# A fused two-layer block with routed experts: shared feed-forward moved out of the loop, last batch in half banks and token tiles, and three programs joined into one

## The chip, the cores and the metric

One NeuronCore of one Trainium2 chip runs the whole kernel in one launch. The metric is the device time of that launch in microseconds (us), median over runs. All data are fp32 except a few small bf16 tiles that hold exact integers or split values. The engines are named as in the profile: PE is TensorE (PEld its weight loads), DVE is VectorE, ACT is ScalarE, POOL is GpSimd, SP is SyncE. SP, ACT and POOL also issue DMAs from queues of their own.

## The reference, cut to what matters

The input `x` is 8 batches of 256 tokens with 512 features. Four blocks follow each other; `ln` is a layer norm without weights.

```python
x = x + tanh(g_xattn[0]) * L0_xattn(ln(x), ctx, ctx)   # retention: scores summed over all 8 batches
x = x + tanh(g_ffn[0])   * L0_ffn(ln(x))               # shared FF + one expert times a weight
x = x + tanh(g_xattn[1]) * L1_xattn(ln(x), ctx, ctx)   # softmax attention, 8 heads
x = x + tanh(g_ffn[1])   * L1_ffn(ln(x))               # 64 experts, top 6, capacity 256
```

In the first block `A = maximum(abs(masked.sum(axis=0)), 1)` needs the scores of every batch before any batch can go on. The last block, on which most of the change bears, is

```python
su = x_flat @ w_shared_up
y_s, g_s = split(su, 2, axis=-1)
shared = silu(g_s) * y_s @ w_shared_down
scores = sigmoid(x_flat @ w_gate)
_, topk_idx = top_k(scores, 6)
w = take_along_axis(scores, topk_idx, -1); w = w / w.sum(-1, keepdims=True)
# place of each (token, expert) pair among the rows of its expert, in token order; rows past 256 are dropped
out_r[e] = (silu(g_r) * v_r) @ w_down[e],  g_r, v_r = split(x_disp[e] @ w_up[e], 2)
routed = sum over the 6 experts of a token of w * out_r
result = shared + routed
```

## The kernel before

The work is three programs one after the other, each with tiles of its own and a barrier of all engines behind it.

**`setup_and_scores`** normalises `x` batch by batch, stores the transposed result and the values to DRAM (`xnT_d`, `v_d`), accumulates the scores of all batches in PSUM and makes `AT`, the masked `A`. SP loads the weights behind the last loads of this part: `weights(...)`.

**`main_loop`** takes a batch through four streams of units: F (first block's output, gate, and the first feed-forward), T (softmax attention), R (routing and the shared feed-forward of the last block) with its sends. Every engine walks one written list, `ORDER`, in which `T.S0+1` means that unit T.S0 lags one step behind: in step s it works on batch s-1. There are 8 steps with a new batch and 3 more in which the lagging streams finish (lags go up to 3). Every engine runs its own units of that list strictly in order, with semaphores between engines. PSUM has one group of four banks, `quad`, three banks in rotation, `work`, and one bank `pV`. `quad` holds a chunk of attention scores: first in the units T.S0 to T.S7 (PE makes 128x2048 scores, DVE takes the row maxima, L888), then in T.Q0 to T.Q7 (PE makes them again, transposed and shifted, ACT takes the exponentials into `probs`, L721). T.V are the products with the values (L1178). POOL sums the exponentials of a group of four chunks (T.sum, L624, three sums of four instructions each, twice a batch), a matmul T.Z turns that into row sums, and DVE scales (T.A), POOL adds (T.add). R then does: stats, norm, turn, gates (routing logits), sigmoid, hot (top 6 as one-hot), pos (places by a matmul), slots, places (addresses); POOL sends 12 groups of 128 rows per batch to the experts' row table `xs_d` (R.x, L644) and 12 groups of row numbers to `ids_d` (R.send, L658). The shared feed-forward is R.up (eight matmuls of 128x256, L1057), R.shared (one exponential on ACT, four DVE instructions, L935 to L938), R.down (two matmuls of 128x512, L1221, and two DVE instructions, L943), and SP stores the sum to `acc_d`. ACT also issues the 56 fills that clear `xs_d` and `y_d`.

**`experts`** takes 32 pairs of experts: rows and weights are loaded four pairs ahead (L1290, L123, L124), PE transposes the rows (L1435), makes the up product (L1447) and the down product (L1458), ACT and DVE evict, and POOL scatters the results to `y_d` by the numbers in `ids_d` (L1340). POOL first sends the last batch's 12 groups of numbers (L1329); SP waits for them, loads `e_ids` (L1311) and only then the rows and weights of pair 4. At the end, for each of 16 token tiles, SP loads two halves of 768 KB from `y_d` (L1306), DVE adds six scaled slices into `acc` (L1415), and ACT stores the tile (L1374).

## Time and profile before

| | us |
|---|---|
| median of 3 runs (lowest, highest) | 1253.87 (1252.85, 1258.54) |
| the profiled execution's own time | 1244.85 |
| its span, first to last instruction | 1243.1 |
| PE busy | 1003.2 (81%) |
| DVE busy | 707.4 (57%) |
| POOL busy | 611.1 (49%) |
| ACT busy | 300.8 (24%) |

The profile is of one execution, whose time lies 0.7% below the median of the others. Busy time is summed over the whole span; the stages have different limits, so the stages are read one by one. POOL's share does not count the time in which it issues a DMA beyond the instruction itself. An fp32 matmul of the program shows as two PE instructions in the trace.

### The profile page before, as it was taken

To read this page: it belongs to the slowest core of one execution; us is meant where nothing else is said; L and a number is where in the kernel's file an instruction comes from. 1 tells how busy PE (TensorE), PEld (TensorE's weight loads), DVE (VectorE), ACT (ScalarE), POOL (GpSimd) and SP (SyncE) were. 2 spreads that over 40 slices of the span, in tenths; PEclk is the share of its full clock that TensorE was granted. 3 is DMA by queue.
4 is the path that set the end of the run, shared out by engine and by line. 5 is a ranking of instruction groups with operands and counts; after the bars stand their busy time and mean duration, and the time that the engine had idled before them with its cause. 6 is when DMAs were issued, how large, how long until landed. Compare 5 with 4: busy or idle time off the path is not lost. (4 is left out here: it accounts for less than half of the span.)

```text
span 1243.1 us, 16070 instructions
## 1 busy us (share of the span) xinstructions
PE 1003.2 (81%) x5966; PEld 562.1 (45%) x5966; DVE 707.4 (57%) x1241; ACT 300.8 (24%) x390; POOL 611.1 (49%) x588
## 2 busy tenths in 40 slices
PE   6947989999999999999999966742888989899000
PEld 6945545454555545545555422231454555455000
DVE  3312353778868778778687785450333333333598
ACT  2411022223232222242322312200223232323000
POOL 1100004626777668667776687875443444344100
PEclk9978999999999999999999986765999999999655
DMA  4892049487380652712403015035789899994796
GB/s 183 304 356 85 1 163 385 180 294 282 136 305 12 233 196 102 273 67 102 136 2 127 27 51 187 0 131 200 251 304 330 291 344 296 328 297 172 281 419 283
DMA packets 103834, 252.24 MB, mean 203 GB/s; under 512 B 14016, under 2 KB 14400, under 8 KB 102993
## 3 DMA queue, kind: packets, MB, share of 16 engines
q1 hardware_dynamic: 50896, 137.92, 32.1%
q10 hardware_dynamic: 31872, 62.92, 13.3%
q0 software_dynamic: 20992, 50.42, 10.6%
q8 instruction: 46, 0.75, 0.3%
q14 instruction: 28, 0.22, 0.1%
HBM read 125.26 MB, written 134.33 MB: 209 GB/s over the span
## 5 line engine op out<-in xcount | busy, mean ns | idle before, releaser
L1340 POOL DMA_INDIRECT y_d<-e_eo,e_ids x128 | 124.8, 975 | 158.5 <-DVE e_eo L1395 126.8
L624 POOL TENSOR_TENSOR t_psum<-t_psum,t_probs 128x512 f32<-128x512 f32 x128 | 162.8, 1302 | 50.8 <-ACT t_probs L721 47.8
L888 DVE TENSOR_REDUCE t_nmx<-quad 128x4 f32<-128x2048 f32 x64 | 146.5, 2289 | 62.6 <-PE quad L1138 62.4
L721 ACT ACTIVATE t_probs<-quad 128x2048 f32<-128x2048 f32 x64 | 120.2, 1877 | 174.6 <-PE quad L1163 174.4
L644 POOL DMA_INDIRECT xs_d<-r_norm,r_xaddr x96 | 95.5, 995 | 28.0 <-issue 27.7
L658 POOL DMA_INDIRECT ids_d<-r_tokk,r_addr x84 | 82.7, 984 | 42.5 <-DVEq L1003 20.9
L1160 PE MATMUL quad<-b_qry,b_key 32*128 32x512 f32 x512 | 78.8, 687 | 19.9 <-ACT t_probs L721 13.6
L1389 DVE TENSOR_TENSOR e_hT<-e_pU,e_gate 128x256 f32<-128x256 f32 x32 | 13.6, 425 | 140.5 <-ACT e_gate L1356 98.2
L1435 PE MATMUL e_pT<-ident,e_xg 128*128 128x128 f32 x512 | 72.4, 286 | 22.9 <-DMA e_xg<-xs_d 22.4
L624 POOL TENSOR_TENSOR t_psum<-t_probs 128x512 f32<-128x512 f32 x64 | 82.3, 1320 | 11.7 <-ACT t_probs L721 9.7
L1138 PE MATMUL quad<-b_key,b_qry 32*128 32x512 f32 x512 | 74.7, 654 | 16.4 <-DVE t_nmx L888 13.2
L605 POOL TENSOR_TENSOR f_rstd<-f_veps,mhalf 128x2 f32<-128x2 f32 x24 | 17.0, 707 | 144.3 <-DVE f_veps L789 144.3
L1435 PEld LDWEIGHTS e_pT<-ident,e_xg 128*128 128x128 f32 x512 | 56.7, 144 | 61.0 <-issue 26.8
L1178 PE MATMUL t_pV<-t_probs,b_cT 128*32 128x512 f32 x512 | 68.2, 620 | 0.0
L1384 DVE COPY e_xT<-e_pT 128x512 f32<-128x512 f32 x64 | 44.1, 689 | 41.0 <-PE e_pT L1435 39.6
L1057 PE MATMUL work<-f_normT,wupT 128*128 128x256 f32 x256 | 61.3, 395 | 0.0
L1057 PE MATMUL work<-b_xnT,wg 128*128 128x256 f32 x256 | 59.7, 387 | 1.6 <-DVE f_zT L808 1.6
L1395 DVE COPY e_eo<-e_pD 128x512 f32<-128x512 f32 x64 | 44.3, 692 | 28.5 <-PE e_pD L1458 25.8
L1049 PE MATMUL work<-wo,f_zT 128*128 128x512 f32 x128 | 58.6, 601 | 1.3 <-issue 1.3
L1049 PE MATMUL work<-wexp,f_normT 128*128 128x512 f32 x128 | 58.7, 601 | 0.5 <-issue 0.5
L1049 PE MATMUL work<-wdnT,f_hT 128*128 128x512 f32 x128 | 58.8, 604 | 0.0
L1057 PEld LDWEIGHTS work<-f_normT,wupT 128*128 128x128 f32 x256 | 48.9, 196 | 17.0 <-issue 10.6
(185 smaller groups left out, 1657.8 us busy)
## 6 DMA issues: line engine op xcount, KB each, us to landing
xs_d<-zero ACTq DMA_DIRECT2D x32, 1024.0 KB, 8.1
e_xg<-xs_d SPq DMA_DIRECT2D x32, 1024.0 KB
y_d<-zero ACTq DMA_DIRECT2D x24, 1024.0 KB
e_xg<-y_d SPq DMA_DIRECT2D x16, 768.0 KB, 11.5
e_eo<-y_d SPq DMA_DIRECT2D x16, 768.0 KB, 11.7
a_x<-in_x SPq DMA_DIRECT2D x8, 512.0 KB, 4.5
a_cT<-in_ctxT SPq DMA_DIRECT2D x8, 512.0 KB, 3.6
v_d<-a_val SPq DMA_DIRECT2D x8, 512.0 KB, 2.7
```

Source lines behind the costliest of these rows:

```text
L624: ins = g_.tensor_tensor(psum0[:, q, :], first[:, q, :], probs[s % NP][:, q, :], ALU.add)
L644: g_.indirect_dma_start(out=xs_d, out_offset=bass.IndirectOffsetOnAxis(ap=xaddr[b % 2][:, t, k:k + 1], axis=0), in_=normR[b % 2][:, t, :], ...
L658: g_.indirect_dma_start(out=ids_d, out_offset=bass.IndirectOffsetOnAxis(ap=addr[b % 2][:, t, k:k + 1], axis=0), in_=tokk[b % 2][:, t, k:k ...
L721: A(probs[s % NP][:, :, :], quad[:, :, :], ACT.Exp, scale=SCALE1).then_inc(W["exp_ok"], 1)
L888: V.tensor_reduce(nmx[g][:, m, :], quad[:, :, :], axis=AX.X, op=ALU.max, negate=True).then_inc(W["mx_ok"], 1)
L1049: ins = mm(dst, lhs[:, k, t * P:(t + 1) * P], w[:, k, :], start=(k == 0), stop=(k == KC - 1))
L1057: ins = mm(dst[:, j * S:(j + 1) * S], w[:, k, o * P:(o + 1) * P], rhs[:, k, :], start=(k == 0), stop=(k == KC - 1))
L1138: ins = mm(quad[:, q, :], qry[b % 2][r, g, m * P:(m + 1) * P], key[b % 2][r, g, :], start=True, stop=True)
L1160: mm(quad[:, q, :], key[b % 2][r, g, n * P:(n + 1) * P], qry[b % 2][r, g, :], start=True, stop=False)
L1178: ins = mm(pV[q * HD:(q + 1) * HD, :], cT[:, n, r:r + HD], probs[s % NP][:, q, :], start=(n == 0), stop=(n == KC - 1))
L1340: g_.indirect_dma_start(out=y_d, out_offset=bass.IndirectOffsetOnAxis(ap=ids[:, HC * p + n:HC * p + n + 1], axis=0), in_=eo[u][:, n, :], i ...
L1435: last = tr(pT[t][:, k * P:(k + 1) * P], xg[u][:, HT * e + t, k * P:(k + 1) * P], ident[:, :])
```

## The change

1. **Shared feed-forward out of the loop.** The units R.up, R.shared and R.down leave the list. The transposed normalised rows of batches 0 to 6 are kept in DRAM (`nrT_d`, unit R.keep, a 512 KB store per batch) and loaded back (7 x 512 KB) near the end. Eight units L.up0 to L.up7 at the end of the list make the up products into the `quad` banks; ACT applies Silu and DVE multiplies (one instruction each per batch) into `shT`. The down product is made in the final sum: one 128x512 matmul per token tile.
2. **The final sum.** PE takes the first three of the six slices of a tile: it multiplies them by diagonal matrices (`diag`, made by ACT from the identity, three 128x128 instructions per tile) into the PSUM bank in which the shared product is. DVE takes the other three and then adds the bank.
3. **The last batch.** Steps 0 to 5 follow a new `ORDER`; what comes after is a second written list, `ENDING`. In it the attention of batch 7 works on halves of `quad` (L.S0a, L.S0b, ...: two banks each), the sums of its exponentials are made by PE in a bank of `work` (four more matmuls per L.V) and not by POOL, and its routing goes by token tile (L.stats0, L.norm0, ..., L.places1, L.rows0, L.rows1).
4. **One program.** The three parts share one block and one address map (`arena`, `put`, `banks`) without barriers; waits on single semaphores take their place. Parts that stand for the barriers: ACT and DVE wait for the accumulated rows' stores (`accst`) before the experts, SP waits for the last sends (`xscat`, `scat`) before it loads rows, PE for `shT_ok` before the first up product.
5. **Order on the queues.** SP issues the loads for batch 0 (`load_front`) ahead of the weights, and all weights but the routing ones ahead of the stores of batches 6 and 7. The sends of a batch's row numbers wait for a semaphore of their own (`ids_ok`), and those of batch 6 stand behind the last rows of batch 7.

The diff, cut to its core:

```diff
+            start = nc.sbuf_base
+            sb("arena", [P, 123 * 256], ctx=mid)
+            put = lambda n, shape, kb, d=F32: nc.alloc_sbuf_tensor_at(n, shape, d, offset=start + int(1024 * kb))
+            banks = mid.enter_context(nc.psum_tensor("banks", [P, 2 * KC, D], F32))
...
+            parts = [setup_and_scores(nc, io, outer, mid, everything)]
+            parts.append(main_loop(nc, io, outer, mid, everything))
+            parts.append(experts(nc, io, out, outer, mid, everything))
+            with nc.Block() as block:
...
+        sp.dma_start(mask[:, :, :, :], io["mask"]).then_inc(mask_in, 16)
+        for u in range(2):
+            sp.wait_ge(stored[u], 2 * 16)
+        v["load_front"](sp, 0)
+        weights("gate_in", "wg", "gamma", "beta")
+        weights("wo_in", "wo")
+        weights("ffn_in", "wg0", "wupT", "wdnT", "wexp")
+        last = NB // 2 - 1
...
+T.sum1a/5 T.sum1b/5 T.V2/5 T.Z0/5 T.V3/5 T.add0/5 T.Q7/5 T.A0/5 F.out0/7 T.S0/6 F.keys/7 F.out1/7 F.stats/7 T.V4/5 T.S1/6 F.norm/7 T.V5/5
...
+T.Q5/6 R.places/5 F.down1/7 T.V2/6 T.Q6/6 T.Z0/6 T.V3/6 T.Q7/6 F.stats3/7 F.norm3/7 T.V4/6 T.sum1a/6 T.V5/6 T.A0/6 L.S0a/7 L.S0b/7 T.V6/6
+T.sum1b/6 L.S1a/7 L.S1b/7 T.sum1c/6 L.S2a/7 L.S2b/7 R.x3/4 T.add0/6 L.S3a/7 L.S3b/7 T.Z1/6 L.P0/7 L.S4a/7 R.acc/5 R.acc/6 L.S4b/7 R.send0/5
+R.x0/5 T.V7/6 L.M0/7 L.S5a/7 L.S5b/7 L.Q0a/7 T.A1/6 L.Q0b/7 L.S6a/7 T.add1/6 L.S6b/7 R.stats/6 R.send1/5 L.Q1a/7 R.norm/6 L.Q1b/7 L.S7a/7
+R.x1/5 R.x2/5 L.S7b/7 R.send2/5 R.turnA/6 R.send3/5 R.turnB/6 L.Q2a/7 L.Q2b/7 R.gates/6 L.add0/7 L.M1/7 L.Q3a/7 L.P1/7 L.V0/7 R.sigmoid/6
+L.V1/7 R.x3/5 R.hot/6 L.A0/7 L.Q3b/7 R.slots/6 L.stats0/7 R.places/6 L.V2/7 L.Q4a/7 R.x0/6 L.V3/7 L.Q4b/7 L.norm0/7 R.x1/6 L.Q5a/7 L.A1/7
+R.pos/6 L.Q5b/7 L.add1/7 L.sigmoid0/7 L.stats1/7 L.hot0/7 L.V4/7 L.norm1/7 R.x2/6 L.Q6a/7 L.slots0/7 L.Q6b/7 R.keep/5 L.V5/7 R.x3/6 L.Q7a/7
+L.Q7b/7 L.places0/7 R.keep/6 L.V6/7 L.rows0/7 L.rows1/7 L.V7/7 R.send0/6 L.turn0/7 R.send1/6 R.send2/6 L.sigmoid1/7 L.gates0/7 L.pos0/7
+L.turn1/7 R.send3/6 L.gates1/7 L.up0/7 L.up1/7 L.hot1/7 L.pos1/7 L.up2/7 L.up3/7 L.up4/7 L.up5/7 L.up6/7 L.up7/7 L.slots1/7 L.places1/7
...
+        def r_keep(b):
+            sp.wait_ge(W["x4T_ok"], 2 * b + 2)
+            sp.dma_start(nrT_d[b, :, :].rearrange("p (k s) -> p k s", k=KC), normRT[:, :, :]).then_inc(W["nr_kept"], 16)
...
+        def last_weighted(s):
...
+                for q in range(G):
+                    r = (g * G + q) * HD
+                    mm(pV[q * HD:(q + 1) * HD, :], cT[:, n, r:r + HD], probs[s % NP][:, q, :], start=(n == 0), stop=(n == KC - 1))
+                for q in range(G):
+                    ins = mm(z[q * HD:(q + 1) * HD, :], ones32[:, :], probs[s % NP][:, q, :], start=(n == 0), stop=(n == KC - 1))
...
+        def shared_up(c):
+            def stage(b):
+                if c == 0:
+                    pe.wait_ge(W["nr_in"], 16 * LB)
+                    pe.wait_ge(W["exp_ok"], 8 * b + 16)
                 pe.wait_ge(W["x4T_ok"], 2 * b + 2)
+                since(pe, W["shT_ok"], c - G + 1)
+                by_features(quad[:, c % G, :], wsu, normRT if c == LB else nrT[c], 0).then_inc(W["su_mm"], 1)
+            return stage
...
+        for u in range(2):
+            sp.wait_ge(W[f"xscat{u}"], 16 * T * TOPK * (NB // 2))
+        sp.wait_ge(W["pv_mm"], 8 * NB)
+        for p in range(XB):
+            load_rows(p)
+        for u in range(2):
+            sp.wait_ge(W[f"scat{u}"], 16 * T * TOPK * (NB // 2 - u))
+        sp.wait_ge(ids_sent, 16 * T * TOPK)
...
+        def halves(i):
+            j = 2 * i
+            u = j % (XB + OB)
...
+            since(pe, part_ok, i - HC + 1)
+            mm(pD[i % HC][:, :], shT[:, i // T, (i % T) * P:(i % T + 1) * P], wsd[:, :], start=True, stop=False)
+            pe.wait_ge(part_in[u], 16 * uses(j, XB + OB))
+            pe.wait_ge(diag_ok, i + 1)
+            for k in range(HALF):
+                last = mm(pD[i % HC][:, :], diag[i % 2][:, k, :], parts[u][:, k, :], start=False, stop=(k == HALF - 1))
+            last.then_inc(half_mm, 1)
```

## Rows read from the trace of the kernel before

**Rows 1.** Busy time by stretch: start:end, length, busy us, granted clock, DMA share, GB/s.

```profile
78.60:147.90 69.30, 49.89 (x177) 34.53 (x178) 12.48 (x29) 5.80 (x10) 1.99 (x4) 0.81 0.30 116
...
384.70:467.70 83.00, 81.48 (x477) 42.43 (x473) 63.71 (x116) 23.39 (x26) 59.95 (x55) 1.00 0.46 165
...
632.80:717.50 84.70, 83.09 (x492) 43.02 (x492) 66.05 (x118) 24.63 (x28) 62.08 (x57) 1.00 0.17 57
717.50:798.00 80.50, 59.60 (x344) 22.33 (x336) 52.02 (x85) 20.94 (x18) 63.76 (x56) 0.75 0.25 92
798.00:866.30 68.30, 21.71 (x65) 12.93 (x61) 23.75 (x61) 3.74 (x6) 46.01 (x46) 0.58 0.35 129
866.30:1161.20 294.90, 254.65 (x1792) 147.72 (x1792) 100.01 (x160) 85.19 (x160) 132.62 (x136) 0.98 0.83 284
1161.20:1243.10 81.90, 0.00 (x0) 0.00 (x0) 70.83 (x96) 0.00 (x0) 0.00 (x0) 0.50 0.89 359
```

**Rows 2.** Timeline at the end of setup: start us, us, engine, line, operation.

```profile
77.08 1.02 DVE L336 TENSOR_SCALAR AT<-mask 128x1024 f32<-128x1024 f32 x2
...
78.60 0.33 SPq L561 DMA_DIRECT2D b_val<-v_d  x1
...
89.94 1.43 PE L1067 MATMUL work<-b_val,AT 128*128 128x128 f32 x5 [16.50 <-DMA b_val<-v_d]
```

**Rows 3.** Timeline of PE in one step of the loop.

```profile
393.00 3.72 PE L1057 MATMUL work<-r_normT,wsu 128*128 128x256 f32 x16
396.65 1.14 PE L1138 MATMUL quad<-b_key,b_qry 32*128 32x512 f32 x8
...
419.13 1.02 PE L1221 MATMUL work<-wsd,r_shT 128*128 128x512 f32 x2
420.08 1.14 PE L1160 MATMUL quad<-b_qry,b_key 32*128 32x512 f32 x8
...
454.99 3.70 PE L1049 MATMUL work<-wdnT,f_hT 128*128 128x512 f32 x8
```

**Rows 4.** Groups of POOL's instructions in one step, 384.7 to 467.7 us.

```profile
L624 POOL TENSOR_TENSOR t_psum<-t_psum,t_probs 128x512 f32<-128x512 f32 x16 | 20.5, 1312 | 4.8 <-ACT t_probs L721 4.5
L644 POOL DMA_INDIRECT xs_d<-r_norm,r_xaddr x12 | 12.1, 1008 | 3.3 <-issue 3.3
```

**Rows 5.** Costliest groups of the page: busy us, mean ns, idle before.

```profile
L888 DVE TENSOR_REDUCE t_nmx<-quad 128x4 f32<-128x2048 f32 x64 | 146.5, 2289 | 62.6 <-PE quad L1138 62.4
```

**Rows 6.** Timeline of DVE, routing of the last batch, first and last row.

```profile
823.59 0.46 DVE L949 TENSOR_SCALAR r_eg<-r_eg 128x128 f32<-128x128 f32 x1 [2.86 <-issue]
...
835.36 0.48 DVE L1005 TENSOR_SCALAR comb_all<-r_small,r_wsum,tg_f 128x6 f32<-128x6 f32 x2 [0.15 <-issue]
```

**Rows 7.** Timeline, last send of rows to second expert pair, and one stretch.

```profile
850.13 0.98 POOL L644 DMA_INDIRECT xs_d<-r_norm,r_xaddr  x1 [0.30 <-issue]
...
856.00:858.00 2.00, 0.00 (x0) 0.00 (x0) 0.00 (x0) 0.00 (x0) 0.00 (x0) 0.50 0.00 0
...
860.50 2.84 SPq L1290 DMA_DIRECT2D e_xg<-xs_d  x4
...
866.26 3.87 PE L1435 MATMUL e_pT<-ident,e_xg 128*128 128x128 f32 x16 [22.44 <-DMA e_xg<-xs_d]
871.00 3.67 PE L1447 MATMUL e_pU<-e_xT,wo 128*64 128x256 f32 x32 [0.88 <-issue]
...
883.84 0.44 PE L1447 MATMUL e_pU<-e_xT,wupT 128*64 128x256 f32 x2
```

**Rows 8.** The final sum: timeline, one stretch of 5 us, time to landing of the output.

```profile
1158.58 0.98 POOL L1340 DMA_INDIRECT y_d<-e_eo,e_ids  x1 [0.30 <-issue]
...
1165.89 6.21 DVE L1415 SCALAR_TENSOR_TENSOR e_acc<-e_xg,comb_all,e_acc 128x512 f32<-128x512 f32 x8 [11.20 <-DMA e_xg<-y_d]
...
1185.00:1190.00 5.00, 0.00 (x0) 0.00 (x0) 4.73 (x7) 0.00 (x0) 0.00 (x0) 0.50 1.02 419
...
DMA to landing us min/median/max: 2.0/6.7/7.5
```

2378 lines of the change are left out of this document (1286 added, 1092 removed), and 3 rows, old and new, of the table RELEASES.

## Prediction

> **What bounds the kernel now.** I cut the busy time into stretches that follow the program [rows 1]; what to see is which engine is full in each. In a full step of the loop (384.7 to 467.7) PE is busy 81.5 of 83.0 us at the full clock: PE is the bound, DVE (64) and POOL (60) are not. Step 0 (78.6 to 147.9) and the drain (717.5 to 866.3) are different: PE is busy 49.9, 59.6 and 21.7 us of 69.3, 80.5 and 68.3, and the granted clock averages 0.81, 0.75 and 0.58, so part of that busy time is at the 1.2 GHz level. In the drain POOL is the busiest engine (110 of 149 us). The experts (866.3 to 1161.2) keep PE busy 86% and the DMA engines 83%. The final sum has DVE busy 71 of 82 us and PE idle. All sums are made against the profiled execution: 1244.85 us, of which the span is 1243.1.
>
> **Term 1, end of setup.** DVE finishes `AT` at 78.1, but PE's first product starts at 89.94, because the first load of a batch is issued at 78.60 behind the weights [rows 2]. In the change this load stands ahead of the weights, and its wait (stores of batches 0 to 3) was met long before, so nothing queues behind it for long. 89.9 - 78.2 = 11.7 us go. The new step 0 transposes before it makes the first gate product (3.65 us), which so far covered the wait for the norm: I give back 2 us, half of it. **-9.7** (bounds -12 and -5).
>
> **Term 2, shared feed-forward out of the steps.** R.up holds PE from 393.00 to 396.65, 3.65 us; R.down from 419.13 to 420.08, 0.95 us, twice [rows 3]: 5.55 us per batch. By the end of F of batch 7 (717.5) these units had run for batches 0 to 4 in the old list. Adding up the units on either list up to that point with such rows gives PE 24.5 us less in the new one. What DVE sheds (some 5 us per batch) is off the path. The added stores (7 x 512 KB out and in) meet DMA engines that are busy 0.17 to 0.53 here; R.keep makes SP wait for the transposed rows in mid-step, and behind it stands the load for the next batch, wanted some 40 us later: nothing. POOL is busy 60.0 us in a step [rows 1], and each of its 24 sends holds it 0.30 us beyond its 0.98 [rows 7]: 67 us, which the change leaves as they are, against a step of 82.8 - 5.55 = 77.2. PE stays the bound. **-24.5** (bounds -28, and +7 if the new order leaves more gaps). F of batch 7 then ends at 717.5 - 9.7 - 24.5 = 683.
>
> **Term 3, the drain.** Before, it is 153.5 us from 717.5 to the first up product at 871.0 [rows 7]. In it engines and DMA queues also stand still before the barrier opens at 860.5: nothing is moved from 856 to 858. After, three queues have to be followed.
> POOL: after F of batch 7 its list holds three sums of four instructions (12 x 1.31 = 15.7 [rows 4]), 11 groups of three sends (33 x 1.28 = 42.2) and four adds and three roots (7, from the 5 us that a step's two adds and four roots leave of its 60) before the second tile's root: 65 us. So that root is not before 683 + 66 = 749.
> DVE: its list up to the last attention scaling adds up to 48 us, of which 16 half maxima at half of 2.29 us [rows 5]. PE must fit 16 half-scores, 16 half-exponentials and the V units of 2 us around them, part of it at 1.2 GHz; I take 59 us for the last V, 742, and scaling and add bring it to POOL's bound. From 749: norm, hot, slots, places of tile 0 and sigmoid of tile 1 on DVE. Two tiles took 12 us [rows 6], one tile then some 8 us: 758. The second tile's hot ends at 761.
> PE: gates of the second tile 755.5, then two shared up products, 7.3 us, stand ahead of L.pos1: it runs at 764. Slots, places: 767. Six sends, 7.7: 775. Landing and load of the first rows: 2.7 (1158.58 to 1161.2) and 5.7 (860.5 to 866.2) give 783. But PE has eight up products of 3.65 = 29.2 us behind 755.5, and starts them cold: 787. Transposes, 2 us: the first expert product at **789**. 789 - 683 = 106 against 153.5: **-47.5**. Bounds: POOL's queue alone (88 us to the last row, plus 10.4) ends at 782, -54; with all eight up products at 1.2 GHz, as PE ran much of this stretch before, +29, so -18.
>
> **Term 4, the experts.** Before, they start at half clock: the first interval between up products is 12.8 us (871.0 to 883.84), later ones average 8.9 ((1158.58 - 883.84) / 31). After, dense products stand right ahead: -4. Against it: the numbers of batches 6 and 7, 24 sends of 1.28, are sent only after the last rows, so SP is free to load pair 4 at 775 + 31 + 2 = 808. PE wants those rows in pair 3, at about 789 + 3 x 8.9 + 4 = 820, the load takes 5.7: hidden, but the DMA engines start with less lead, and the share was 0.83 over the whole stage. +1. **-3** (bounds -4, and +8 if the transfers run late for a while).
>
> **Term 5, the final sum.** Before: 84.5 us from the last scatter (1158.58) to the end. DVE does six slices in 4.67 us per tile (1165.89 on: 8 instructions of 0.75 in 6.21), 95% busy. The DMA engines, though, are also full: share 1.02, 419 GB/s [rows 8]. The loads (32 x 768 KB) and stores (16 x 256 KB) are 29.4 MB, 70.1 us at that rate: begun at 1161.2 they end at 1231.3 at best. DVE's new work is four instructions of 0.75 to 0.78, 3.1 us per tile, PE's 4 products of 0.92 = 3.7 us [rows 3], both under 4.4 us of transfers. After the last landing three slices, the bank's add (3.2 us), issue and landing of a store (2.4): 1237.3 against 1243.1, **-5.8**. So the halved DVE work buys little. Bounds: -16 if transfers were free and PE set the pace; +15 with PE's clock mixed as in the drain. The Trainium skill ("DMA: Bandwidth & Descriptors", Where 436 GB/s comes from) puts the limit for transfers between HBM and SBUF at about 358 GB/s per core. By that figure this sum would take 82 us of transfers and the tail would be 6 us longer than before instead of shorter; the 419 GB/s of the row speak against it.
>
> **Sum.** -9.7 - 24.5 - 47.5 - 3 - 5.8 = -90.5: 1244.85 becomes 1154.4, a ratio of 0.927. The runs lie above the profile (median 1253.87), and I expect the same after: 1253.87 x 0.927 = **1162 us**.
>
> **Rivals.** (a) *The steps gain nothing*: in the tighter step POOL's 67 us in strict order, between exponentials and roots that others wait for, become the bound and a step stays near 82.8. For it: POOL would be 87% taken. Against: it waits little now [rows 4]. Term 2 goes: 1187.
> (b) *More is gained*: POOL's queue alone bounds the drain (-54 in place of -47.5), and the new order fills waits of the first steps too: PE waits 19 us in step 0 [rows 1], of which 12 might go. For it: DVE's list in the drain is only 48 us. Against: step 0 has one batch in flight, and nothing new to fill it. 1143.
> (c) *The final sum becomes PE's*: PE is idle from 1154 to the first landing and starts it at 1.2 GHz; if it stayed there, 16 tiles x 7.4 = 118 us in place of 70: +48, 1210. Against: step 0 began as cold and averages 0.81 with PE busy 72% [rows 1], so the clock came back there under less work than 3.7 of 4.4 us.
> (d) *Slower than before*: the new order starves PE. In 717.5 to 798 PE got through 59.6 x 0.75 = 45 us of full-clock work in 80.5 us. If the full steps ran like that, a step would take 77.2 / 0.56 = 138 us and the kernel over 1500. It decides from 13 us of extra waiting per step over seven steps, a step of 90 us. Against: now PE waits 1.5 us per step, with the same dependencies and one unit fewer to wait for.
> (e) *The transfers of the final sum slow down*: the experts' stage moves 284 GB/s at a share of 0.83, 342 at a full share [rows 1], since rows are written there too. PE's reads and the stores now lie closer to the loads. At 342 the 29.4 MB take 86 us in place of 70: +16, 1178. The Trainium skill's figure of 358 ("DMA: Bandwidth & Descriptors", Where 436 GB/s comes from) would make a case of this kind. Against: the stores were there before, at 419 GB/s.
> (f) *Joining the programs does nothing*, because the wait from 851 to 860.5 is the landing of the last rows and not the barrier: a 256 KB scatter lands in 2.7 us elsewhere [rows 8], and from 856 on nothing moved [rows 7], so it is not; if some of it stays, +5, inside the range.
>
> **Chances.** Forecast 0.62 (its own range 1140 to 1182), (a) 0.12, (b) 0.13, (c) 0.05, (d) 0.03, (e) 0.05. The range 1130 to 1195 leaves out (c), (d) and the edges of the rest, 2 in 10 at most. A difference under 0.5% cannot be told from none in this kernel. Faster by more than that: 0.96; same 0.01; slower 0.03.
>
> **What would show it.** In the profile after: the first product of the loop near 78; steps of 77 us with PE busy above 95%; F of batch 7 over near 683; the second tile's sends over near 775 and the first expert product near 789 with PE at 1.00; interval of 8.9 from the first pair; in the final sum a DMA share of 1.0 and 4.4 us per tile with DVE and PE both under 90%. The prediction is wrong if steps exceed 80 us, if PE waits at L.pos1 or L.up0 for more than 10 us, or if the final sum shows PE at 0.50.

## The result, and the profile after

The kernel after takes 1290.40 us (median of 4 runs, 1279.61 to 1296.55) beside 1255.84 us for the kernel before (4 runs, 1252.85 to 1258.54): a ratio of 1.027, 95% interval 1.023 to 1.031. It is slower, where 1162 us was forecast. Its profiled execution took 1293.52 us, of which the span is 1291.8. (The 1253.87 us further up are the median of three of these four runs.)

The stages, in us, cut at the same events in both traces (start of F.out0 of a batch, end of F of batch 7, first expert up product, last scatter, end). "Drain" is what lies between the end of F of batch 7 and the experts; the seven steps are steps 0 to 6:

| stage | before | after | difference | forecast |
|---|---|---|---|---|
| to the first product of the loop | 89.9 | 78.5 | -11.4 | |
| seven steps | 542.9 | 589.6 | +46.7 | |
| rest of F of batch 7 | 84.7 | 92.6 | +7.9 | |
| to the end of F of batch 7, sum | 717.5 | 760.7 | +43.2 | -34.2 |
| drain, to the first up product | 153.5 | 151.8 | -1.7 | -47.5 |
| experts | 287.6 | 298.0 | +10.4 | -3 |
| last scatter to the end | 84.5 | 81.3 | -3.2 | -5.8 |

What the page says of the whole (busy time, and the shares of the chain that ended last):

```profile
PE 1085.9 (84%) x6109; PEld 593.4 (46%) x6110; DVE 680.2 (53%) x1197; ACT 314.2 (24%) x446; POOL 582.4 (45%) x565
...
PE 45%; another core or an unknown queue 16%; DVE 11%; POOL 9%; issue 8%; DMA 6%; ACT 4%; SPq 0%; ACTq 0%; POOLq 0%; DVEq 0%
```

There is no other core. The 16% are waits on a semaphore whose update came long after the instruction that makes it had ended by the trace: the waits marked "remote" below. Such an update is called a late completion here. In the kernel before they were 5%.

One full step, and five microseconds of the final sum, busy time by stretch (columns as in [rows 1]):

```profile
490.40:579.30 88.90, 79.60 (x457) 39.83 (x453) 63.88 (x110) 22.92 (x24) 60.28 (x55) 0.96 0.44 160
...
1240.00:1245.00 5.00, 4.25 (x10) 1.75 (x11) 3.52 (x6) 0.98 (x3) 0.00 (x0) 1.00 1.01 417
```

PE has 20 instructions fewer than in the step of [rows 1], and still the step is 88.9 us in place of 83: PE is idle 9.3 us of it, and part of the rest is at the lower clock (the granted clock averages 0.96, and PE is busy 79.60 us where the same work takes 76.29 at 1.00 in e4 below). The final sum is as forecast: the DMA engines full, PE and DVE not.

The middle of that step, timeline of POOL, PE and DVE:

```profile
529.69 1.30 POOL L715 DMA_INDIRECT xs_d<-r_norm,r_xaddr  x1 [0.20 <-issue]
...
535.79 1.95 PE L1212 MATMUL banks<-wg,f_normT 128*128 128x8 f32 x16
...
537.59 6.38 PE L1220 MATMUL banks<-f_normT,wupT 128*128 128x256 f32 x27
...
544.06 0.97 POOL L715 DMA_INDIRECT xs_d<-r_norm,r_xaddr  x1 [0.30 <-issue]
...
545.05 4.92 POOL L703 TENSOR_TENSOR t_psum<-t_probs,t_probs 128x512 f32<-128x512 f32 x4
...
546.44 0.25 DVE L954 MAX8 f_m<-banks 128x8 f32<-128x8 f32 x2 [6.92 <-remote]
546.72 3.27 DVE L956 TENSOR_TENSOR f_gap<-f_m 128x2 f32<-128x2 f32 x1
...
551.21 0.61 PE L1362 MATMUL banks<-ident,t_nmp 128*128 128x128 bf16 x4 [4.30 <-DVE t_nmp L1026]
```

PE makes the logits (L1212) by 537.74. DVE waits for nothing else and starts on them at 546.44, 8.7 us later. All that time POOL is in one run of 12 sends, 529.69 to 545.03, and 1.4 us after its end the completion is there. DVE then takes 3.27 us to subtract 128x2 numbers, while POOL adds (in m1 below such a subtraction takes 0.16 us when POOL is silent), and PE waits 4.30 us behind both. The same pattern ahead of the experts:

```profile
877.53 3.62 PE L1220 MATMUL banks<-r_normT,wsu 128*128 128x256 f32 x16
881.47 1.07 PE L1693 MATMUL banks<-ident,e_xg 128*128 128x128 f32 x8 [0.32 <-DMA e_xg<-xs_d]
...
884.84 0.38 ACT L885 ACTIVATE r_shT<-banks 128x256 f32<-128x256 f32 x1 [9.58 <-remote]
...
903.38 0.97 POOL L1577 DMA_INDIRECT ids_d<-r_tokk,r_addr  x1 [0.30 <-issue]
...
908.70 0.38 ACT L885 ACTIVATE r_shT<-banks 128x256 f32<-128x256 f32 x1 [23.48 <-remote]
...
909.62 1.75 PE L1693 MATMUL banks<-ident,e_xg 128*128 128x128 f32 x7 [27.09 <-ACT e_xT L1597]
```

The last shared product starts at 877.53 and ends by the page at 881.15; ACT gets it at 908.70, after a run of 30 sends from 866.36 to 904.36. PE stands still for 27 us, at the experts' first transposes, which wait for a copy of ACT that stands behind this one in ACT's list.

### The profile page after: what moved, and what is told of

Its sections match the earlier page's. It is cut to its first block, busy times and chain, and to the rows that moved or that the text cites. A ratio compares the mean times of both kernels' runs of the same rounds, so it can differ in the third digit from the quotient of the medians.

```text
span 1291.8 us, 16371 instructions
## 1 busy us (share of the span) xinstructions
PE 1085.9 (84%) x6109; PEld 593.4 (46%) x6110; DVE 680.2 (53%) x1197; ACT 314.2 (24%) x446; POOL 582.4 (45%) x565
## 4 chain that ended last, share of the span: by engine, by line
PE 45%; another core or an unknown queue 16%; DVE 11%; POOL 9%; issue 8%; DMA 6%; ACT 4%; SPq 0%; ACTq 0%; POOLq 0%; DVEq 0%
PE banks L1212 12%; POOL t_psum L703 7%; PE banks L1220 6%; DMA e_eo<-y_d 5%; PE banks L1716 5%; PE banks L1693 3%; PE banks L1375 3%; PE banks L1305 2%; PE banks L1705 2%; DVE t_nmx L1004 2%; PE banks L1319 1%; PE banks L399 1%; ACT e_eo L1607 1%; PE banks L393 1%
## 5 line engine op out<-in xcount | busy, mean ns | idle before, releaser
L1004 DVE TENSOR_REDUCE t_nmx<-banks 128x4 f32<-128x2048 f32 x56 | 127.9, 2285 | 54.1 <-PE banks L1305 33.1
L806 ACT ACTIVATE t_probs<-banks 128x2048 f32<-128x2048 f32 x56 | 105.1, 1877 | 149.5 <-PE banks L1378 123.6
L1693 PE MATMUL banks<-ident,e_xg 128*128 128x128 f32 x512 | 70.8, 282 | 27.7 <-ACT e_xT L1597 27.1
L1305 PE MATMUL banks<-b_key,b_qry 32*128 32x512 f32 x448 | 67.0, 668 | 18.6 <-DVE b_qry L994 10.6
L1375 PE MATMUL banks<-b_qry,b_key 32*128 32x512 f32 x448 | 69.4, 691 | 7.9 <-ACT t_probs L806 3.9
L703 POOL TENSOR_TENSOR t_psum<-t_probs,t_probs 128x512 f32<-128x512 f32 x56 | 71.4, 1309 | 8.7 <-ACT t_probs L806 8.6
L1220 PE MATMUL banks<-f_normT,wupT 128*128 128x256 f32 x256 | 63.5, 398 | 6.2 <-issue 6.0
L1212 PE MATMUL banks<-wdnT,f_hT 128*128 128x512 f32 x128 | 62.0, 631 | 2.9 <-DVE f_xs L971 2.9
L1220 PE MATMUL banks<-b_xnT,wg 128*128 128x256 f32 x256 | 62.4, 400 | 0.0
L1212 PE MATMUL banks<-wexp,f_normT 128*128 128x512 f32 x128 | 62.2, 632 | 0.0
L1212 PE MATMUL banks<-wo,f_zT 128*128 128x512 f32 x128 | 58.6, 601 | 0.9 <-issue 0.9
L1220 PEld LDWEIGHTS banks<-f_normT,wupT 128*128 128x128 f32 x256 | 49.9, 199 | 18.0 <-issue 11.4
```

What stands on the lines that cost most here:

```text
L703: ins = g_.tensor_tensor(psum0[:, q, :], first[:, q, :], probs[s % NP][:, q, :], ALU.add)
L806: A(probs[s % NP][:, :, :], quad[:, :, :], ACT.Exp, scale=SCALE1).then_inc(W["exp_ok"], 1)
L1004: V.tensor_reduce(nmx[g][:, m, :], quad[:, :, :], axis=AX.X, op=ALU.max, negate=True).then_inc(W["mx_ok"], 1)
L1212: ins = mm(dst, lhs[:, k, t * P:(t + 1) * P], w[:, k, :], start=(k == 0), stop=(k == KC - 1))
L1220: ins = mm(dst[:, j * S:(j + 1) * S], w[:, k, o * P:(o + 1) * P], rhs[:, k, :], start=(k == 0), stop=(k == KC - 1))
L1305: ins = mm(quad[:, q, :], qry[b % 2][r, g, m * P:(m + 1) * P], key[b % 2][r, g, :], start=True, stop=True)
```

## The experiments

The runs came in sets; the kernels of one set ran on one chip, each beside the kernel before. The kernel before took:

| set | chip | kernel before, us | late completions |
|---|---|---|---|
| the result | not recorded | 1255.84 | yes |
| m1, e1 to e3 | 13 | 1243.61 | yes |
| m2, e4, e5 | 5 | 1198.40 | no |
| m3, e6 to e8 | 11 | 1196.28 | no |
| e9 to e12 | 2 | 1255.55 | yes |
| e13 to e15 | 2 | 1242.75 | yes |

The last column says whether the traces of the set have "remote" waits. Ratios to the kernel before are compared, and traces only with a look at the set. Each "step" is from one F.out0 to the next; steps 3 to 6 are the full ones, in which all streams run.

**m1_completions**, a program that has only POOL's sends and additions beside dense products. PE makes dense products into four banks, ACT copies each, and DVE runs four small instructions; POOL's part by stage is

```python
if what in ("numbers", "rows"):
    for k in range(24): send(what, k)            # one indirect DMA each
if what == "sums":
    for k in range(24): add(128x512)
if what == "threes":
    for k in range(24):
        send("rows", k)
        if k % 3 == 2: add(); add()
```

> A small program that computes nothing of the block. PE makes 14 dense up products (16 matmul records each, 3.65 us) in each of six stages; ACT copies each product and DVE then runs two maxima, one subtraction of two small SBUF tiles and one 128x512 scaling. From the second product of a stage on POOL does: nothing; 24 sends of 4-byte numbers in a row; 24 sends of rows in a row; 24 additions of 128x512; 24 row sends in threes with two additions behind each three; nothing. Theory A (a long unbroken run of sends holds back the completions of PE): in stages two and three ACT's copies come on time for the first 5 to 9 us of the run and then late by several us, up to the end of the run plus 1 to 4 us; in the stages without sends, and in the one with threes, each copy follows its product within 0.1 us. Rival B (the late completions of the block come from its own order or from its other transfers): all six stages show the same 0.1 us. In both, the subtraction on DVE takes 0.16 us where POOL is silent and may take up to one POOL addition, 1.3 us, where POOL adds.

Busy time in the stages with numbers, rows, sums and threes (the first two up to the first copy that is in time again), then ACT's timeline in the stage with numbers, in which POOL sends from 66.18 to 96.63:

```profile
61.50:105.50 44.00, 34.74 (x131) 26.85 (x130) 6.22 (x32) 4.67 (x8) 24.48 (x25) 0.81 0.02 1
125.80:167.90 42.10, 32.52 (x131) 26.35 (x131) 6.32 (x32) 4.68 (x9) 24.53 (x25) 0.86 0.39 150
189.00:234.30 45.30, 45.30 (x211) 39.89 (x210) 15.09 (x52) 7.76 (x13) 32.69 (x25) 1.00 0.00 1
237.40:282.60 45.20, 45.20 (x210) 39.48 (x208) 18.20 (x52) 7.76 (x13) 35.29 (x33) 1.00 0.29 111
```

```profile
72.27 0.60 ACT L98 ACTIVATE evicted<-banks 128x512 f32<-128x512 f32 x1 [2.86 <-PE banks L129]
77.49 0.60 ACT L98 ACTIVATE evicted<-banks 128x512 f32<-128x512 f32 x1 [4.63 <-remote]
94.38 0.60 ACT L98 ACTIVATE evicted<-banks 128x512 f32<-128x512 f32 x1 [16.30 <-remote]
100.10 1.08 ACT L98 ACTIVATE evicted<-banks 128x512 f32<-128x512 f32 x2 [5.12 <-remote]
105.53 0.60 ACT L98 ACTIVATE evicted<-banks 128x512 f32<-128x512 f32 x1 [4.34 <-PE banks L129]
```

A product takes 3.45 us here. Up to 6 us into the run every copy comes on time; then they are 1.8, 15.2 and 17.5 us late, and the last comes 3.5 us after the run. It is not the completions alone: from 84.54 on, 18 us into the run, PE's own instructions come singly or in twos, with idle time that nothing in the trace explains, in the middle of a product and so without a semaphore to wait for:

```profile
86.66 0.38 PE L129 MATMUL banks<-xT,wsu 128*128 128x256 f32 x1 [0.93 <-issue]
90.86 1.50 PE L129 MATMUL banks<-xT,wsu 128*128 128x256 f32 x2 [1.30 <-issue]
97.17 0.59 PE L129 MATMUL banks<-xT,wsu 128*128 128x256 f32 x1 [2.00 <-issue]
```

The two stages with unbroken runs take 61 and 60 us from first to last product, the others 45.3. Additions alone, and threes with additions between, hold nothing back. DVE follows each copy of ACT within 0.05 us, so ACT's completions are not late. DVE's subtraction takes 0.16 us in silence and up to 1.1 beside additions, but 3.0 where two additions stand between sends, more than the one addition (1.3 us) that was expected. The late completions are as theory A expected, and rival B is refuted for this program.

**e1_spread_sends**: POOL's sends alone are moved, in steps 0 to 5.

```diff
-R.x1+3 R.send2+3 R.x2+3 T.Q1+1 ... R.x3+3 F.turn2B+0 T.sum0a+1 F.norm2+0 R.send3+3 ... T.sum0b+1 F.best+0 ... T.sum0c+1
+R.x1+3 R.send2+3 T.Q1+1 ... F.turn2B+0 T.sum0a+1 F.norm2+0 R.x2+3 ... T.sum0b+1 R.x3+3 F.best+0 ... T.sum0c+1 R.send3+3
```

> The kernel after, with nothing changed but the places of POOL's sends in steps 0 to 5: the run of 12 sends in a row is broken into 6, 3, 3 (each with one sum of four additions between), and the last three go behind the third sum. Theory A (PE's completions are held back by the long run): the wait of DVE for the logits (6.9 us, 'remote') falls under 2 us, PE's wait for the negated maxima (4.3 us) goes, and a full step falls from 89 to 83 us or less; five full steps, so 30 us less in all, about 1260. Rival B (order of PE's and DVE's own units): DVE waits the same, step within 2 us of 89, total 1280 to 1300. Rival C (the added stores, the joined program): the same as B.

1262.52 us, ratio 1.0155 (1.012 to 1.019), below the 1.027 of the kernel after without overlap. Steps 3 to 5 take 88.0, 85.7 and 83.7 us in place of 100.1, 90.4 and 88.9: theory A, though none is down to 83. Moving POOL's instructions and nothing else gave 12, 5 and 5 us. Step 6, whose list is unchanged, takes 95.1 us in place of 88.8: DVE's two scalings for the queries take 6.54 us at its start, beside POOL's additions, and PE waits 5.25 us for them. That effect comes back in e5.

**e2_old_order**: the list of before (less R.up, R.shared, R.down; R.acc behind T.add1, R.keep behind R.turnB) for steps 0 to 5 in the program of after.

> The kernel after, with the written order of the kernel before in steps 0 to 5 (less its shared feed-forward; with the stores of the accumulated and of the transposed rows at the same places), and the same ending. Theory A and rival B both hold the order guilty: a step near 78 us (82.8 less 5.55, plus 1), five full steps 50 us less than in the kernel after, total about 1240. Rival C (added stores, one address map): a step stays over 85 us and the total within 15 us of 1290.

1240.52 us, ratio 0.998 (0.994 to 1.001). Full steps 80.2, 80.4 and 80.3 us. The kernel before takes 82.4 to 83.0 for the same steps in the trace beside the result. So joining, address map and added stores do not keep a step over 85 us (rival C out), and the new order costs some 8.5 us per step (88.8 in the result's last full step and in e12). But the step is not 77.2: PE is busy 76.1 us and waits 4.2, 2.8 for exponentials and 1.4 for maxima. ACT's relu waits 8.4 us ("remote") behind a run of nine sends; that this makes PE's waits was not tested by itself. In e5, without late completions, the best such step waits 2.4 us. Where the old list passes into the new ending one step takes 98.9 us, so the total is worse than the steps.

**e3_before_without_shared**: the kernel before with the three units taken out of the list (the shared feed-forward is not computed).

> The kernel before, with the shared feed-forward of the last block left out altogether (its two products, the exponential and the six DVE instructions of a batch; the accumulated rows are stored as they are). It prices the removal alone. The prediction's term: PE's 5.55 us per batch go, a full step falls from 82.8 to 77.2, and over the eight batches the kernel is 35 to 44 us faster than before. Rival (POOL's queue or the waits take over): a step of 81 us or more, less than 15 us in all.

1233.82 us, ratio 0.992 (0.989 to 0.995): 10 us, not 35 to 44. Full steps 82.0, 82.0, 80.3, 79.9. In the second of them PE waits 2.8 us for exponentials and 1.4 for maxima, where in the kernel before it waited 1.0 for exponentials: some of the removed products had stood where PE otherwise waits. The expectation failed, and with it the price of the second term as a sum of durations. The trace of the kernel before held this already. Its step 2 has no shared products yet (R.up lags three steps), and it takes 78.5 us and not 77.2:

```profile
223.40:301.90 78.50, 76.05 (x456) 38.76 (x452) 60.77 (x110) 22.71 (x25) 38.75 (x34) 1.00 0.71 260
```

**m2_run_lengths, m3_completions_again.** m2 is m1 with other runs; m3 is m1 unchanged, in another set.

> The small program of m1_completions with other stages, all with row sends on POOL from the second of 14 dense products on: 24 in a row; 6; 9; 12; 24 with one tiny fill of a few bytes behind each three; 24 with one addition of 128x512 behind each three; 24 with two additions behind each six; 24 with a tiny fill behind each; 24 where POOL waits after each three until they have landed; 24 in a row; none. Theory A (PE's completions are held back in an unbroken run): late completions in the stages with 24 and 12 in a row, nearly none with 6, 1 to 3 us with 9; none where additions or landings break the run. What a tiny fill does is open: none late if any other instruction breaks the run, as late as in the first stage if POOL must be off the sends for some time. It is also run without a profile: if the held-back completions were made by the profiler, those runs would be shorter than the profiled one by the sum of the losses, some 13 us for each stage of 24 in a row and 5 for 12; if they are the chip's own, the times agree within 3 us.

> The program of m1_completions once more, also without a profile. On a chip where the kernel before takes 1240 us or more: the same losses as in m1 (stages two and three 61 and 60 us long in place of 45), and a total of 348 with and without the profile. On a chip near 1198: all stages with sends 45 us long, a total near 320.

In m2 no completion was late in any of the eleven stages, 24 sends in a row included: 45.3 us each. So it said nothing of lengths. m3 shows that the difference to m1 does not lie in the program; it is the same kernel as m1, and these are its stages with numbers and with rows:

```profile
60.90:106.20 45.30, 45.30 (x211) 39.88 (x211) 10.33 (x52) 7.76 (x13) 25.02 (x25) 1.00 0.02 1
109.30:154.60 45.30, 45.30 (x211) 39.88 (x210) 10.28 (x52) 7.77 (x14) 24.81 (x25) 1.00 0.37 139
```

It takes 316.99 us in place of 348.28, and its runs with and without the profile lie within 316.2 to 318.0.

**e4_after_again, e6_before_again, e12_after_third_chip**: the two kernels unchanged, in other sets.

> The changed kernel once more, so that it stands beside the others on one chip: 1.02 to 1.03 times the kernel before.

> The kernel before once more, for its trace on another chip. On the chip of m2_run_lengths to e5_old_order_six the held-back completions were absent and the kernel before took 1198 us; on the two chips before that they were there, at 1243 and 1256. Theory A': the behaviour belongs to the chip, and is the difference. If this chip shows a time near 1198, no instruction of the trace waits for a late completion of PE ('remote'); if it shows 1240 or more, ACT's relu in each full step does, by 8 us, and the first expert products again.

> The changed kernel beside the others of this call: 0.99 of the kernel before on a chip where that takes under 1210 us, 1.02 to 1.03 where it takes over 1240.

e4: 1186.99 us, ratio **0.990** (0.987 to 0.994); its trace has no "remote" wait. e12: 1287.90, ratio **1.027** (1.024 to 1.030). e6: 1199.62 in its one run, no "remote" wait either. So the change gains 1% where the completions come in time, and loses 2.7% where they don't. The late completions alone do not hide the forecast gain of 7%: without them the kernel is still 77 us short of the forecast, and 53 of these lie in term 2. The expectation of e4 was wrong because it took the effect to be everywhere. The stages where they come in time, before (e6) and after (e4):

| stage | e6, before | e4, after | difference |
|---|---|---|---|
| to the first product | 91.6 | 78.7 | -12.9 |
| seven steps | 536.5 | 564.4 | +27.9 |
| rest of F of batch 7 | 83.8 | 89.8 | +6.0 |
| drain | 146.8 | 110.7 | -36.1 |
| experts | 254.4 | 259.8 | +5.4 |
| last scatter to the end | 84.8 | 80.9 | -3.9 |

A full step of each (e6 first, then e4) and, in e4, the stretch with the shared products that in the result's trace led to the stop of 27 us:

```profile
465.30:546.70 81.40, 81.23 (x477) 42.43 (x473) 66.89 (x116) 23.42 (x26) 59.44 (x55) 1.00 0.46 169
```

```profile
478.10:560.60 82.50, 76.29 (x456) 39.24 (x453) 67.46 (x110) 22.83 (x24) 60.16 (x55) 1.00 0.47 172
818.00:843.00 25.00, 24.43 (x121) 21.02 (x120) 7.61 (x26) 3.88 (x9) 17.14 (x18) 1.00 0.64 231
```

PE has 4.9 us less to do per step, and waits 6.2 us where it waited 0.2: among others 2.1 for POOL's last sum of exponentials, 1.6 for DVE's maxima and 1.4 for rows that DVE makes in stream F. Before the experts it now goes through.

Most of the +27.9 us of the seven steps does not lie in these full steps. Step by step, e4 takes 61.9, 80.3, 82.1, 89.6, 85.5, 82.5 and 82.5 us where e6 takes 56.9, 75.4, 78.6, 81.4, 81.4, 81.4 and 81.4: some 22 us come in steps 0 to 3, while the pipeline fills. Part of that is work moved forward (in step 1 PE is busy 2.9 us more), and in step 3 it is a wait that is followed under term 2 below; the rest was not taken apart.

**e5_old_order_six, e7_sends_before_sum, e8_best_of_parts**, in sets without late completions.

```diff
 e5, against e2:  -R.send2+3 R.send3+3 ... R.x3+3 ... T.sum0b+1 T.sum0c+1      +R.send2+3 R.send3+3 ... T.sum0b+1 R.x3+3 T.sum0c+1
 e7, against e5:  -T.V2+1 R.send0+2 T.Q6+1 F.stats3+0 F.norm3+0                +T.V2+1 T.Q6+1 F.stats3+0 F.norm3+0 R.send0+2
```

> As e2_old_order, but three of the nine sends that POOL makes in a row in a full step are moved behind the next sum, so that no run of a full step is longer than six. Theory A: ACT's late relu of the second up product (8.3 us, 'remote') comes on time, PE's 2.8 us of waiting for exponentials go, and a full step falls from 80.3 to 77.5 us, the 77.2 of the forecast; 10 to 14 us less in all. Rival (the shared products had covered waits of 3 us that are there whatever POOL does): a step stays at 80.

> As e5_old_order_six, but POOL makes three sends between the last root of a step and the sum that follows it, so that POOL is not adding when DVE makes its two 128x512 scalings for the queries. In e5 these scalings took 5.6 us in place of 1.1 to 3 in two of three full steps, behind POOL's four additions (4.9 us), and PE waited 4.2 and 1.0 us. Theory: the scalings take 1.1 us each time, PE's two waits go, and the full steps that took 84.5 us take 78 to 80; 10 us less in all than e5. Rival: POOL is behind by then, the sum comes 4 us later, the exponentials wait for its buffers, and a step stays at 84.

> e7 with the old order carried on through the seventh step, the written ending from there on, and in the ending three sends each moved behind the third sum and into POOL's idle 11 us before the last root of batch 7. Expected from the parts: the step at the seam (88 to 99 us) falls to 80, the rest as e7: 15 us less than e5_old_order_six, a ratio to the kernel before of 0.965 on a chip without late completions and 0.98 on one with them.

e5: 1174.62 us, ratio 0.979 (0.977 to 0.982). Its first full step takes 78.5 us, the next two 84.5 and 84.9, so one step of three came near the expected 77.5. The trace shows one difference, here in the second (POOL's addition, DVE's scalings for the queries, PE):

```profile
369.66 0.75 POOL L676 TENSOR_TENSOR f_rstd<-f_veps,mhalf 128x2 f32<-128x2 f32 x1
370.36 4.93 POOL L704 TENSOR_TENSOR t_psum<-t_probs,t_probs 128x512 f32<-128x512 f32 x4
370.44 5.60 DVE L995 TENSOR_SCALAR b_qry<-f_xs,f_mv,f_rstd 128x512 f32<-128x512 f32 x2 [1.40 <-POOL f_rstd L676]
...
382.44 2.09 PE L1306 MATMUL banks<-b_key,b_qry 32*128 32x512 f32 x8 [4.21 <-DVE t_nmx L1005]
```

POOL's four additions start 0.08 us ahead of DVE's scaling, and DVE is done only when they are. In the step of 78.5 us DVE was 0.02 us ahead and took 3.0 us. The Trainium skill ("SBUF — State Buffer", SBUF: two separate sides) says that GpSimd and a DVE instruction in a two-port mode, or with two SBUF inputs, share a port pair as an exclusive lock: whichever starts first has it for its whole instruction. The trace agrees in who waits, with the addition that here all four additions in a row went first. Such a long stretch on DVE beside POOL's additions is called a lock-out below. e7: 1178.38, ratio 0.983 (0.978 to 0.987). The scalings now take 1.0 us, as expected, but the steps take 81.2, 82.9 and 84.3 us, near the rival's 84: the lock-out moved to the next small instruction, and PE waits 4.26 us as before:

```profile
377.32 4.95 POOL L704 TENSOR_TENSOR t_psum<-t_probs,t_probs 128x512 f32<-128x512 f32 x4
...
378.29 4.02 DVE L906 TENSOR_SCALAR f_veps<-f_mv 128x2 f32<-128x2 f32 x1
```

e8, with the old order through step 6 and so without the long step at the seam between old list and new ending (88.0 us in e5): 1174.38, ratio 0.980 (0.976 to 0.985), steps of 81.2 to 84.1. Expected was 0.965; the lock-out of 4.0 us stands in three of its steps.

**e9_after_fewer_sums, e10_old_order_fewer_sums, e11_sum_behind_scaling**, in a set with late completions. e9 and e10 leave out three of four of POOL's additions, so the row sums hold old values for three of four heads; only the times of these two kernels are of use.

```diff
-                for q in range(G):
+                for q in range(G if b == 0 and g == 0 else 1):        # e9 in after, e10 in e5
...
+                if g == 1 and n == 1 and b + 1 < NB - 1:              # e11
+                    pool.wait_ge(W["q_ok"], b + 2)
```

> The kernel after, with three of the four additions of each of POOL's sums of exponentials left out after the first sum (the row sums of the softmax then hold old values for three of four heads of a group). POOL's additions fall from 31 to 8 us per step. If DVE's lock-out and POOL's lateness make the excess: full steps of 77 to 79 us. If PE's and DVE's own order in the new list makes it: over 81 us still.

> e5_old_order_six with the same additions left out. In both theories the full steps, 78.5 to 84.9 in e5, all take 77 to 78.5: the forecast's 77.2 with what PE waits for ACT. If they stay at 84 the lock-out is not their cause.

> e5's order in the loop, the seam and the ending of e8, and POOL waits, before the first sum of the second head group, until DVE's scalings for the queries are done (about 1.1 us, behind a root that POOL has just made). e7 and e8 showed that a wait of 3.8 us only moves the lock-out to the next small DVE instruction. Theory: the scalings take 1.1 us, all full steps take 78.5 us as the best one of e5 did, total 20 us under e8, a ratio to the kernel before of 0.965 on a chip without late completions. Rival: as in e7 the lock-out moves to another instruction, and the steps stay at 83 to 84.

e9: 1262.84 us, ratio 1.006 (1.004 to 1.008); e10: 1241.13, 0.988 (0.985 to 0.992). A full step of each:

```profile
476.70:562.50 85.80, 81.00 (x456) 40.81 (x452) 55.03 (x110) 22.79 (x24) 37.01 (x37) 0.94 0.46 166
```

```profile
367.40:446.40 79.00, 76.08 (x457) 38.87 (x453) 55.37 (x110) 23.10 (x25) 36.95 (x37) 1.00 0.50 180
```

With the same work the old order takes 79.0 us and the new one 85.8. POOL's additions cost the new order 3 us per step (88.8 in e12), its own order and the run of 12 the rest, 6.8 us. In e10 the step at the seam takes 102.1 us, so its ratio says little of its steps. e11: 1239.88, ratio 0.988 (0.985 to 0.992), steps 78.4, 78.4, 81.0, 81.3, 79.9. The wait of one microsecond on POOL keeps the scalings at 1.0 us in steps 1 to 6, and no 128x2 instruction of DVE takes over 1.5 us there: the lock-out is gone. Where a step takes 81 us, PE still waits 2.3 to 2.6 us for maxima; why is open. The expected ratio of 0.965 was for a chip without late completions, and e11 was not run on one.

**e13_gated_numbers, e14_best_gated, e15_best_again**, in a set with late completions. POOL's last 24 sends of numbers come in fours, behind PE's progress; e14 is e11 with that, e15 e11 itself.

```diff
+        gates = [(W["su_mm"], NB), (up_mm, 1), (dn_mm, HT), (up_mm, 2), (dn_mm, 2 * HT), (up_mm, 3)]
+        for j in range(2 * T * TOPK):
+            if j % 4 == 0:
+                pool.wait_ge(*gates[j // 4])
```

> The kernel after; the 24 sends of row numbers of batches 6 and 7, which stood in one run behind the last rows, are made in six groups of four, each behind a completion of PE (the last shared product, then up and down products of the first three pairs), and SP loads the numbers behind the loads of pairs 4 and 5. On a chip with late completions: theory A says that PE's stop of 27 us before the experts goes to under 5 us, the first expert product comes 20 us earlier, and the kernel is 15 to 22 us faster than after (ratio 1.01); the rival (a wait for stores or zeroing) leaves it. On a chip without them PE does not stop there (0.3 us in e4), and the change is within 3 us of nothing or costs some.

> e11 with the same groups of four. On a chip with late completions 15 to 20 us under e11, a ratio of 0.975; on one without within 4 us of e11, about 0.975.

> e11_sum_behind_scaling once more, beside e14: 0.988 of the kernel before on a chip with late completions; on one without 0.975, as its full steps should be 78.5 to 81 us where e5's and e8's were 78.5 to 85.

e13: 1267.73 us, ratio 1.019 (1.017 to 1.022), still slower than the kernel before, but less so than the 1.027 of after. The stop before the experts is gone, but not all its worth is kept; PE at both places:

```profile
876.19 1.07 PE L1697 MATMUL banks<-ident,e_xg 128*128 128x128 f32 x8 [0.20 <-DMA e_xg<-xs_d]
877.58 1.21 PE L1697 MATMUL banks<-ident,e_xg 128*128 128x128 f32 x8 [0.33 <-ACT e_xT L1601]
879.67 3.67 PE L1709 MATMUL banks<-e_xT,wo 128*64 128x256 f32 x32 [0.88 <-DVE e_xT L1644]
...
940.79 2.08 PE L1720 MATMUL banks<-wo,e_hT 64*128 64x512 f32 x4 [11.91 <-DVE e_hT L1649]
```

The first up product comes at 879.7 (905.3 in e12). But the scatters of the first four pairs, held up by the later numbers, now go out in a run of 16 from 917.19, and PE waits 11.91 us behind that one. e13 also moves SP's load of the numbers behind the rows and weights of pairs 4 and 5, so the edit is not the broken run alone; the late completion ahead of the experts is what it removes. The gain is 10 us by the ratios and not 15 to 22. e14: 1223.03, ratio **0.982** (0.980 to 0.985), 3.5 us below e15 (1226.52, 0.986, 0.983 to 0.990), with overlapping intervals: of the 15 to 20 us that were expected from the groups of four at most a few came. e14 has the lowest time with late completions and is faster than both kernels, but is not told apart from e15; e5 (0.979) and e8 (0.980) are the best measured without.

## Why the prediction was wrong, point by point

**What bounds the kernel** was read rightly for the full steps: PE. What was passed over: in the kernel before ACT's relu waits 8 us "remote" in each full step, and the chain of what ended last has 5% "another core or an unknown queue" on a chip where one core runs. That was the mark of the effect that decided the result.

**Term 1, -9.7**: right. -11.4 to the first product, and step 0 is 1.6 us longer (59.6 against 58.0): -9.8. The close hit has some luck in it: e4 against e6 gives -12.9 and +5.0, -7.9.

**Term 2, -24.5: the step that failed.** It reads "PE stays the bound" and "now PE waits 1.5 us per step, with the same dependencies and one unit fewer to wait for". PE's work fell about as computed (81.23 to 76.29 us, 4.9 where 5.55 was taken); its waits didn't stay. In a full step three things came, in this order of size. Their sizes are differences between sets; they add up to 11.5 us, and 88.8 less 77.2 is 11.6.

(1) The new list makes POOL send twelve times in a row, and on some chips completions of PE are then held back: 88.8 us in e12 against 82.5 in e4, 6.3 us per step; e1 breaks the run and gets 5 back.

(2) The order of PE's, DVE's and POOL's units against each other: without late completions the new order takes 82.5 where the old takes 78.5 in its step without a lock-out (e5; 84.5 and 84.9 in those with one), 4.0 us. POOL's additions have a part in it, 2.1 us of PE's waits in e4 being for them; e9 puts the additions, lock-out and queue together, at 3 us per step in a set with late completions. How it divides without them was not measured.

(3) The removed products had covered waits: 82.7 us before, 80 to 82 in e3, and not 77.2; at best the old order comes to 78.4 (e10, e11; 78.5 in e5, and in step 2 of the kernel before), 1.2 above the sum.

Steps 1 and 2 are not full ones and are 4.8 and 3.0 us longer as well; 2.8 us of that is work of PE that the new list makes a step earlier; the rest is open. And one wait was missed altogether. R.x0 lags two steps in place of three, so POOL waits for the fills of `xs_d` for 8.72 us at 298.78, and has the root, the sum and DVE's scaling (6.53 us, where it takes 2.9 in the later steps) behind it:

```profile
298.78 1.18 POOL L715 DMA_INDIRECT xs_d<-r_norm,r_xaddr  x1 [8.72 <-DMA xs_d<-zero]
...
303.31 6.53 DVE L994 TENSOR_SCALAR b_qry<-f_xs,f_mv,f_rstd 128x512 f32<-128x512 f32 x2 [6.40 <-POOL f_rstd L675]
...
309.89 2.09 PE L1305 MATMUL banks<-b_key,b_qry 32*128 32x512 f32 x8 [7.95 <-DVE b_qry L994]
```

PE waits 7.95 us behind it. In e4, where the same wait is 9.28 us, step 3 takes 89.6 us and the later ones down to 82.5, so it is worth some 7 us once; with late completions on top step 3 takes 100.1. The prediction followed what the moved stores wait for, and not what this moved send waits for. (It also took the DMA share as 0.17 to 0.53 where the stores go; in step 2 it is 0.71. Nothing came of that here.)

**Term 3, -47.5**: the three queues were followed rightly, as e4 shows: 110.7 us from the end of F to the first expert product, where 106 was forecast. The last sends of rows end at 97.5 us (forecast 92), because the second tile's root comes at 70.8 us and not 66, and then PE's eight shared up products are the longer queue, as forecast. The gain there is 36.1 us, 11.4 short of the forecast: 4.7 because the drain of after is 110.7, and 6.7 because that of before is 146.8 on such a chip and not 153.5. In the set of the result nothing came of it (-1.7). Four runs of 6 to 30 sends hold completions back, the last stops PE for 27 us, and e13, which breaks that run, takes the stop away. L.pos1 and L.up0, where the prediction looked for a wait of over 10 us, were the wrong place to watch; PE stood still behind L.up7, at the experts' first transposes.

**Term 4, -3**: outside its bounds (-4 to +8) in the result, +10.4, inside without late completions, +5.4. In e4 the first pair does run at the later pace (7.8 us). Then PE waits 4.9 us for the rows of the seventh pair, and that interval is 15.3 us, 7.5 over the pace: the loads lag because SP was free to go on with pair 4 late, which the prediction saw and priced at +1. In the result the pairs took 9.28 us each after the first eight, 8.78 before. The waits point to the cause: ACT waits "remote" for the up products' completions 25 times, 117.5 us in all, in the kernel before 12 times and 58.5 us, in e4 and e6, where the pairs take 7.8 us in both kernels, never. Why twice as often was not tested.

**Term 5, -5.8**: right in mechanism, -3.2 and -3.9 (its own parts, 1231.3 + 3.2 + 2.4, end at 1236.9 and not 1237.3). The transfers run at 417 GB/s and 1.01, and PE is at full clock: rivals (c) and (e) did not come, and the Trainium skill's 358 GB/s ("DMA: Bandwidth & Descriptors", Where 436 GB/s comes from) is not what bounds this sum on one active core.

**Rivals.** (a) named a time near that of the removal alone (e2, e3: 80 to 82), but not its mechanism: POOL is busy 60 us of these steps, and PE waits for maxima and exponentials. (b) counted 19 us of waiting in step 0; 11.3 of these are the wait for the first load, which term 1 had taken already, and from 89.9 on PE waits 8.1. (d), slower with steps of 90 us, is what came, in size and place; it was given 0.03, because its "against" looked at the dependencies, while the list of POOL's instructions was only added up and not followed in its order. (f) did not come: without late completions PE waits 0.3 us at the joint. The range 1130 to 1195 holds the time in neither kind of set once it is scaled: 0.901 to 0.953 of the kernel before, against 0.990 and 1.027. That the 1187 us of e4 lie inside it is the faster chip.

## What to carry to other kernels

When the bound engine is 98% busy, the duration of the work taken from it is what can be gained at most. What that work covered, the waits of the units beside it, has to be read too; a step of the pipeline in which that work is still missing, like step 2 here, shows it. When a list in strict order is rewritten, write out the sequence of each engine by itself, the one that only issues transfers above all, and look for long unbroken runs and for lags that became shorter than a first-time wait. A wait on "another core" in a program of one core is not explained by the program's own order, and wants a small program of its own before anything is forecast over it.

## What the runs showed of the hardware

**Completions of PE are held back behind a long run of indirect DMAs on POOL, in some sets and not in others.** The semaphore updates come late first. In m1 updates due up to 6.1 us (numbers) and 9.6 us (rows) into a run came within 0.4 us, and the next, due at 9.5 and 13.1 us, did not; in the loop the logits, due at 8.0 us, were late, and in the drain a run of six sends (7.4 us) held some back. The last is there 1.3 to 4.3 us after the run. Deeper in the run, from 18 and 20 us on in m1, PE's own instructions come one by one with up to 2.0 us between them. Completions of ACT were not late in m1. It was there in the result's set and in three on chips 13 and 2 (kernel before at 1243 to 1256 us), and absent in the two on chips 5 and 11 (1198 and 1196). m1 and m3, the same program, are 348.28 and 316.99 us; e4 and e12, the same kernel, 0.990 and 1.027. The unprofiled runs of e4 and e12 differ as the profiled ones do, so it is not the profiler's. No chip showed both, and chip 2 showed it twice, so it looks like a property of the chip; with four known chips, and work of neighbours unseen, that is not settled, nor is what holds PE back. Two additions behind each three sends, and a POOL that waits for PE, broke it; what the shortest break is stays open, because m2 fell into a set without the effect. The kernel before is 4 to 5% faster where it is absent. Its experts' stage takes 254.4 us there against 287.6, and its 58.5 us of "remote" waits on up products are gone; that is a comparison of two chips, not an experiment.

**DVE is held up by several of POOL's additions in a row**: 5.60 us for two scalings that take 1.0 us when POOL is silent (e11), 4.02 us for a 128x2 instruction of 0.17. In e5 DVE took 3.0 us where it started 0.02 us ahead of POOL and 5.60 where it started 0.08 us behind.
